# Layer norm shared between GpSimd and VectorE, value weights split first, first transposes row by row, and 28 transposes of the identity ahead of them, in a banded-attention block with a feed-forward network

## Chip, cores and metric

The kernel runs on one core of a Trainium2 chip. The metric is device time in microseconds (us); lower is better.

## The reference

The input x has 8 batches of 1024 rows of 512 numbers, in float32. Each row is normalised (no scale or shift), and two branches are added to x:

```python
xn = (x - mean) / sqrt(var + 1e-5)
Q, K, V = xn @ Wq + bq, xn @ Wk + bk, xn @ Wv + bv        # 16 heads of 64
scores = Q @ K.T; scores = where(|i - j| <= 64, scores, 0.0)
attn = softmax(scores) @ V                                 # zeros outside the band count in the softmax
s = xn @ Win + bin_                                        # 64 units
g = (relu(s[..., None] * W1 + b1) * W2).sum(-1) + b2       # 16 inner units each
out = x + attn @ Wo + bo + g @ Wout + bout
```

## The kernel before

Five engines run five hand-written instruction streams that meet only in semaphores. TensorE (PE) does matmuls and 128x128 transposes, ScalarE (ACT) and VectorE (DVE) empty PSUM, GpSimd (POOL) works SBUF to SBUF, SyncE (SP) issues all DMAs. Matmul operands are split in a high part (a rounded copy, made by ACT) and a low part (the difference, made by DVE from PSUM or by POOL from SBUF); each product is three matmuls (`PASSES`).

**Steps.** The heads are worked in 8 pairs. Step n = 8 b + k works on batch b, pair k: `project` makes the value line (V, halves 0 and 1) and the query and key lines (`project_qk`, Q and K of two halves), while the attention of the pair before (j = n - 1: scores, mask, exponentials, weights, `weigh_values`) and the output projection of the pair before that (o = n - 2, `project_out(0)` to `(7)`, L1027 to L1040) run between them. There are 64 steps and two that drain. The order within a step is written out by hand for each engine; an engine waits in order, so whatever stands behind a waiting instruction waits too.

**Opening.** SP loads the first four row tiles of batch 0 in two quarters (`x_quarter`), the value weights of pair 0, the other four row tiles as one piece (`x_in[1]`), the query and key weights, and then 18 small constants. DVE takes statistics (L701, L681) and aggregates them (`mean_and_variance`, L683). POOL's `layer_norm` (L308 to L323) makes var + eps, its power of -1/2 (L315, rstd), mean times rstd and its negative (shift), four small operations with waits between them. ACT's `normalise` (L413, L422) makes each row tile as xn = rstd x + shift. PE's `transpose_x` (L982) turns four row tiles of one of four column blocks into a PSUM bank (`XT_BANK`), ACT makes the high part of a block (`x_high`), DVE the low part (`x_low`). The order in POOL's stream is: layer norm of tiles 0 to 3, low part of V (`split_low`, L326, L328), layer norm of tiles 4 to 7, low parts of Q and K. In ACT's stream: rows 0 to 3, high part of V, rows 4 to 7, four `x_high`, high parts of Q and K. PE makes blocks 0 and 1, waits for both low parts, makes blocks 2 and 3, waits for all four low parts, and begins V projection 0.

**Weights.** In the first eight steps (`split`) the weights of the next pair are loaded raw, split by ACT and POOL, and written to a DRAM copy (`w_kept`, `wo_kept`); later steps load the split copy. The output weights of pair 7 are an exception: they are never kept, but loaded raw in step k = 7 of each batch and split again in the step k = 0 that follows (ACT L662, POOL L396). In step k = 0 of batches 1 to 7, `project_out(0)` waits for all seven writes or loads of `wo_kept` issued up to then (`wo_got`).

**Layer norm of the next batch.** DVE takes the statistics in steps k = 3 to 5 and aggregates late in step k = 5. POOL's `layer_norm` stands after the second `normalise_weights` and ahead of the weight splits and of `output_low(0)`. ACT makes row tile 0 at the end of step k = 5, between the two `output_high`, the others in steps 6 and 7. **Biases.** POOL adds bo + bout to the rows (`add_biases(p)`, L366 to L371, two tiles each): p = 0 and 1 in step k = 0, p = 2 and 3 in step k = 1, one ahead of the second group of `normalise_weights`, one between the two `output_low`.

**Waits.** Many waits on a count are written twice, once for 1 and once for the count (`in_register`).

## Time and profile before

| | us |
|---|---|
| median of 3 runs | 2365.82 |
| lowest, highest | 2365.38, 2368.52 |
| the profiled execution | 2367.19 |
| its span, first to last instruction | 2365.4 |
| TensorE busy (matmuls) | 2310.1 (98%) |
| VectorE busy | 1960.6 (83%) |
| ScalarE busy | 1576.8 (67%) |
| GpSimd busy | 892.6 (38%) |
| all DMA queues, share of 16 engines | 24% |

The mean granted TensorE clock is 0.996. A busy TensorE is not one at its peak: matmuls overlap in the pipeline, so a matmul is shown as 0.39 us long while the next one starts 0.23 us after it. The waits of an engine are read from the idle time before an instruction and the instruction whose semaphore ended it. "issue" is a wait for which the view finds no releaser. In the rows, L numbers are lines of the kernel before: L1021 projections of Q, K and V, L1038 output projection, L1009 scores, L986 transposes of the rows, L1076 transposes of the attention weights.

### The profile page before, as it was taken

What the parts mean: (1) busy time and instruction counts of PE and PEld (TensorE: products, weight loads), DVE (VectorE), ACT (ScalarE), POOL (GpSimd) and SP (SyncE); (2) the same over time, 40 slices, a digit from 0 to 9 for tenths busy, and PEclk for the clock granted to TensorE, in tenths of its full rate; (3) what the DMA queues carried; (4) which work ended last, traced back from release to release, by engine and by line L of the source; (5) the groups of instructions that cost most, each with busy time, mean ns of one, the idle gap of its engine ahead of it and who ended that gap; (6) DMA issues with size and microseconds to landing.
All of it is one profiled execution on the core that took longest, in us unless ns stands there. A gap on an engine that the chain in (4) does not pass through costs nothing.

```text
span 2365.4 us, 43885 instructions
## 1 busy us (share of the span) xinstructions
PE 2310.1 (98%) x14913; PEld 1975.8 (84%) x14913; DVE 1960.6 (83%) x5088; ACT 1576.8 (67%) x4289; POOL 892.6 (38%) x1302
## 2 busy tenths in 40 slices
PE   5999999999999999999999999999999999999996
PEld 4787888888888888888888888888888888888885
DVE  4887779887898878988889878898879888798886
ACT  3776667666676667666667666766676666676664
POOL 3544435333343324334243332443334332443332
PEclk9999999999999999999999999999999999999999
DMA  4231213221132121421223221331212311122211
GB/s 136 86 125 55 103 59 108 72 72 59 46 123 75 54 75 34 138 65 54 66 63 109 71 57 56 91 98 54 77 46 90 107 55 59 54 89 64 66 47 45
DMA packets 69501, 177.58 MB, mean 75 GB/s; under 512 B 6536, under 2 KB 18848, under 8 KB 69280
## 3 DMA queue, kind: packets, MB, share of 16 engines
q1 hardware_dynamic: 69280, 174.78, 23.6%
q8 instruction: 121, 1.98, 0.3%
q14 instruction: 100, 0.82, 0.1%
HBM read 141.73 MB, written 33.03 MB: 74 GB/s over the span
## 4 chain that ended last, share of the span: by engine, by line
PE 93%; DVE 3%; issue 2%; ACT 1%; POOL 1%; DMA 0%; POOLq 0%; SPq 0%; ACTq 0%; DVEq 0%
PE ps L1021 43%; PE ps L1038 15%; PE ps L1088 12%; PE ps L1076 9%; PE ps L1009 7%; PE ps L1066 2%; PE ps L986 1%; PE ps L1048 1%; DVE probs L733 1%; PE ps L1060 1%; DVE xn L773 1%; DVE v_back L973 0%; ACT probs L449 0%; DVE o_sum L810 0%; DMA acc<-in_L_attn_x 0%
## 5 line engine op out<-in xcount | busy, mean ns | idle before, releaser
L1021 PE MATMUL ps<-xT_hi,w_split 128*128 128x512 f32 x3072 | 1040.7, 400 | 8.1 <-POOL w_split L328 5.0
L358 POOL TENSOR_SCALAR probs<-probs,inv_l,neg_e 128x256 f32<-128x256 f32 x1024 | 569.2, 577 | 638.1 <-DVE neg_e L749 638.1
L1021 PEld LDWEIGHTS ps<-xT_hi,w_split 128*128 128x128 f32 x3072 | 578.4, 188 | 135.3 <-issue 5.2
L449 ACT ACTIVATE probs<-probs,neg_max 128x256 f32<-128x256 f32 x1024 | 507.0, 498 | 142.0 <-DVE neg_max L739 140.9
L1021 PE MATMUL ps<-xT_lo,w_split 128*128 128x512 f32 x1536 | 600.4, 391 | 0.0
L756 DVE TENSOR_TENSOR acc<-ps,acc 128x512 f32<-128x512 f32 x512 | 344.4, 685 | 164.1 <-PE ps L1038 162.6
L500 ACT ACTIVATE pT_hi<-ps 128x512 fp32r<-128x512 f32 x512 | 278.1, 599 | 225.7 <-PE ps L1088 139.5
L364 POOL TENSOR_TENSOR oT_lo<-o_sum,oT_hi 128x512 fp32r<-128x512 f32 x128 | 163.7, 1294 | 682.9 <-ACT oT_hi L516 681.9
L733 DVE CUSTOM_DVE_ANT_0 probs<-ps,mask 128x256 f32<-128x256 f32 x1024 | 372.6, 419 | 31.7 <-PE ps L1009 31.3
L800 DVE TENSOR_TENSOR pT_lo<-ps,pT_hi 128x512 fp32r<-128x512 f32 x512 | 328.2, 684 | 51.1 <-ACT pT_hi L500 50.6
L1038 PE MATMUL ps<-wo_split,oT_hi 128*128 128x512 f32 x1024 | 331.2, 405 | 12.4 <-POOL wo_split L396 5.2
L1021 PEld LDWEIGHTS ps<-xT_lo,w_split 128*128 128x128 f32 x1536 | 290.2, 189 | 51.9
L1088 PE MATMUL ps<-pT_lo,v 128*128 128x256 f32 (+1 forms) x1280 | 306.3, 280 | 0.0
L1088 PE MATMUL ps<-pT_hi,v 128*128 128x256 f32 (+1 forms) x1280 | 302.6, 275 | 0.5 <-DVE pT_lo L800 0.5
L1076 PE MATMUL ps<-ident,probs 128*128 128x128 f32 x2048 | 258.3, 273 | 4.9 <-POOL probs L358 4.0
L1076 PEld LDWEIGHTS ps<-ident,probs 128*128 128x128 f32 x2048 | 230.4, 140 | 23.3 <-issue 3.0
L1088 PEld LDWEIGHTS ps<-pT_lo,v 128*128 128x128 f32 x1280 | 244.1, 191 | 5.1
L1088 PEld LDWEIGHTS ps<-pT_hi,v 128*128 128x128 f32 x1280 | 243.1, 190 | 5.9 <-DVE pT_lo L800 0.8
L1038 PEld LDWEIGHTS ps<-wo_split,oT_hi 128*128 128x128 f32 x1024 | 182.8, 190 | 51.9 <-issue 10.2
L1038 PE MATMUL ps<-wo_split,oT_lo 128*128 128x512 f32 x512 | 201.9, 394 | 0.0
L810 DVE SCALAR_TENSOR_TENSOR o_sum<-ps,v_back,o_part 64x512 f32<-64x512 f32 x256 | 190.8, 745 | 12.9 <-ACT o_part L509 9.0
L449 ACT ACTIVATION_READ_ACCUMULATOR probs<-probs,neg_max 128x1 f32 x1024 | 192.9, 188 | 0.0
(92 smaller groups left out, 3125.1 us busy)
## 6 DMA issues: line engine op xcount, KB each, us to landing
w_split<-w_kept SPq DMA_DIRECT2D x168, 512.0 KB, 3.6
wo_split<-wo_kept SPq DMA_DIRECT2D x49, 512.0 KB, 4.4
out_x<-acc SPq DMA_DIRECT2D x16, 1024.0 KB, 5.9
acc<-in_L_attn_x SPq DMA_DIRECT2D x15, 1024.0 KB, 7.7
w_kept<-w_split SPq DMA_DIRECT2D x24, 512.0 KB, 5.5
wo_raw<-in_L_attn_Wo SPq DMA_DIRECT2D x15, 256.0 KB, 4.8
wo_kept<-wo_split SPq DMA_DIRECT2D x7, 512.0 KB, 3.0
w_raw<-in_L_attn_Wv SPq DMA_DIRECT2D x8, 256.0 KB, 5.5
```

What stands on the lines that cost most here:

```text
L358: pool.tensor_scalar(probs[:, h, t], probs[:, h, t], inv_l[:, c:c + 1], neg_e[:, c:c + 1], ALU.mult, ALU.add).then_inc(normed, 1)
L449: act.activation(probs[:, h, t], probs[:, h, t], ACT.Exp, bias=neg_max[:, c:c + 1], accum_out=row_sum[:, c:c + 1])
L500: act.activation(pT[u % 2][hi][:, c * LINE:c * LINE + LINE], ps[PT_BANK[u][c]][:], ACT.Copy) \
L733: dve.tensor_tensor_reduce(out=probs[:, h, t], in0=ps[SCORE_BANK[tp][h]][:, i * WIN:i * WIN + WIN], in1=mask[:], scale=1.0, scalar=0.0, op ...
L756: dve.tensor_tensor(acc[:, parity, t], ps[OUT_BANK[t]][:], acc[:, parity, t], ALU.add) \
L800: dve.tensor_tensor(pT[u % 2][lo][:, cols], ps[PT_BANK[u][c]][:], f32(pT[u % 2][hi][:, cols]), ALU.subtract).then_inc(pT_lo, 1)
L810: dve.scalar_tensor_tensor(o_sum[half][rows], ps[PV_BANK[u]][rows], v_back[rows], o_part[h][rows], ALU.add, ALU.add).then_inc(o_summed, 1)
L1009: last = pe.matmul(ps[SCORE_BANK[tp][h]][:, i * WIN:i * WIN + WIN], qT[qp][rows, t * P:t * P + P], kT[kp][rows, t * P:t * P + WIN], start= ...
L1021: last = pe.matmul(dst[:], w[wp][:, i, c], xT[xp][:, c, half * LINE:half * LINE + LINE], start=(c == 0 and a == 0), stop=(c == KC - 1 and ...
L1038: last = pe.matmul(ps[OUT_BANK[t]][:], oT[op][:, t * P:t * P + P], wo[wp][:], start=(a == 0), stop=(a == 2))
L1076: last = pe.transpose(ps[PT_BANK[u][c]][:, i % 4 * P:i % 4 * P + P], probs[:, h, t, i % 2 * P:i % 2 * P + P], ident[:])
L1088: last = pe.matmul(ps[PV_BANK[u]][:, q0:q0 + (end - first) * P], v[:, (4 * half + c) % T, h].rearrange("p a d -> p (a d)"), pT[h][part][:, ...
```

## The change

1. **Layer norm.** DVE makes var + eps (in `mean_and_variance`) and shift in one operation (`shift_rows`), POOL only the power (`inverse_deviation`). In batch 0 DVE also makes four of the eight row tiles (`first_rows`: 2, 3, 6, 7), ACT the others. For later batches the power moves in POOL's stream from ahead of the weight splits to behind `output_low(0)` of step k = 5, and DVE's shift stands last in that step.
2. **Opening.** The second half of batch 0 comes in two quarters. ACT splits the value weights before its first row; the high part of Q comes before rows 4 and 5, that of K after them. DVE slips the statistics of tiles 4 to 7 between the four `x_low`. PE transposes row tile by row tile, as the rows come (2, 0, 3, 1), each into four banks, and V projection 0 waits for one block's low part at a time. The mask's first memset moves ahead of the second power.
3. **28 transposes of the identity** stand on PE ahead of the first rows.
4. **Biases.** All four `add_biases` of batch 0 run in step 0.
5. **Output weights.** Those of pair 7 are split once, kept like the others and loaded from the copy; `project_out(0)` of steps up to 9 waits for the split, later ones for their own load; a load waits for the one before it.
6. **Waits** are written once. Helpers that only took register counts go.

```diff
         XT_BANK = (7, 2, 2, 4, 7, 5, 3, 2)
+        FIRST_XT_BANK = (7, 2, 0, 4)
+        WARM_UP = 28
...
             def load_output_kept(n, pair):
                 sp.wait_ge(out_done, T * (n - 1))
+                sp.wait_ge(wo_got, 16 * (n - 1))
                 sp.dma_start(f32(wo_split[:]), wo_kept[pair]).then_inc(wo_got, 16)
...
-            for i in range(2):
+            for i in range(4):
                 sp.dma_start(acc[:, 0, 2 * i:2 * i + 2], x_d[0][:, 2 * i:2 * i + 2]).then_inc(x_quarter[i], 16)
-            load_raw(V_, 0)
-            sp.dma_start(acc[:, 0, 4:T], x_d[0][:, 4:T]).then_inc(x_in[1], 16)
+                if i == 1:
+                    load_raw(V_, 0)
...
-                if k == PAIRS - 1:
-                    load_output_raw(k, PAIRS - 1 + b)
...
-                if attend and k > 0:
-                    load_output_kept(n, k - 1)
+                if n == PAIRS:
+                    keep_output(n, PAIRS - 1)
+                elif attend:
+                    load_output_kept(n, (k - 1) % PAIRS)
...
+            def inverse_deviation(tiles, done):
+                pool.wait_ge(ln_eps, done)
+                pool.tensor_tensor(rstd[:, tiles], var_eps[:, tiles], minus_half[:, tiles], ALU.pow).then_inc(ln_rstd, 1)
...
             pool.wait_ge(pool_set, 2)
-            layer_norm(0, slice(0, 4), 1, 0)
+            inverse_deviation(slice(0, 4), 1)
             split_low(0, V_)
-            layer_norm(0, slice(4, T), 2, 4)
+            pool.memset(mask[:], 1.0).then_inc(pool_set, 1)
+            inverse_deviation(slice(4, T), 2)
             split_low(0, Q_)
             split_low(0, K_)
-            pool.memset(mask[:], 1.0).then_inc(pool_set, 1)
...
                 if attend:
                     normalise_weights(0)
-                if k == 1 and proj:
+                if k == 1 and proj and b > 0:
                     add_biases(2)
                 if attend:
                     normalise_weights(1)
-                if k == 5 and not last:
-                    layer_norm(b + 1, slice(0, T), b + 3, 4 * b + 8)
                 if split_next:
                     split_low(n + 1, V_)
                     split_low(n + 1, Q_)
                 if k == 0 and proj:
                     add_biases(0)
                     add_biases(1)
+                if n == 0:
+                    add_biases(2)
+                    add_biases(3)
                 if attend:
                     output_low(0)
+                if k == 5 and not last:
+                    inverse_deviation(slice(0, T), b + 3)
-                if k == 1 and proj:
+                if k == 1 and proj and b > 0:
                     add_biases(3)
                 if attend:
                     output_low(1)
-                if attend and (split or k == 0):
-                    pool.wait_ge(wo_hi, j + 1 if split else PAIRS - 1 + b)
+                if attend and n <= PAIRS:
+                    pool.wait_ge(wo_hi, j + 1)
...
-            for t in tiles_of(0):
-                normalise(0, t, small=4 if t == 0 else None)
             split_high(0, V_)
-            for t in tiles_of(1):
-                normalise(0, t, small=8 if t == 4 else None)
+            for t in (0, 1):
+                normalise(0, t)
             for i in range(4):
                 x_high(0, i)
             split_high(0, Q_)
+            for t in (4, 5):
+                normalise(0, t)
             split_high(0, K_)
...
             for t in tiles_of(0):
...
-            mean_and_variance(tiles_of(0), 4)
-            for t in tiles_of(1):
                 statistics(0, t)
-            mean_and_variance(tiles_of(1), T)
+            mean_and_variance(tiles_of(0), 4, 1)
+            shift_rows(slice(0, 4), 1)
+            first_rows(2)
+            first_rows(3)
             for i in range(4):
+                statistics(0, 4 + i)
                 x_low(0, i)
+            mean_and_variance(tiles_of(1), T, 2)
+            shift_rows(slice(4, T), 2)
+            first_rows(6)
+            first_rows(7)
...
             pe.wait_ge(ident_set, 1)
-            for i in range(4):
-                if i == 2:
-                    pe.wait_ge(xT_lo, 2)
-                transpose_x(0, i)
+            for i in range(WARM_UP):
+                pe.transpose(ps[V_BANK[0]][:, 0:P], ident[:], ident[:])
+            for t, ready, count in ((2, xn_first, 1), (0, xn_ready, 1), (3, xn_first, 2), (1, xn_ready, 2)):
+                pe.wait_ge(ready, count)
+                for i in range(KC):
+                    last = transpose_tile(0, i, t)
+                    if t == 1:
+                        last.then_inc(xT_done, 1)
...
                     for c in range(KC):
+                        if n == 0 and i == V_ and half == 0:
+                            pe.wait_ge(xT_lo, c + 1)
...
-                    if t == 0 and split:
+                    if t == 0 and o < PAIRS:
                         pe.wait_ge(wo_lo, o + 1)
-                    elif t == 0 and k == 1:
-                        pe.wait_ge(wo_lo, PAIRS - 1 + b)
                     elif t == 0:
-                        pe.wait_ge(wo_got, 16 * (7 * b if k == 0 else 7 * b + k - 1))
+                        pe.wait_ge(wo_got, 16 * (o + 1))
```

## Rows read from the trace of the kernel before

**Rows 1.** Windows of the span: us, busy time and count of each engine, clock, DMA.

```profile
0.00:60.00 60.00, 34.38 (x167) 27.16 (x168) 26.37 (x48) 23.65 (x42) 19.54 (x29) 1.00 0.44 138
350.00:2310.00 1960.00, 1959.55 (x12732) 1680.44 (x12731) 1659.73 (x4338) 1325.95 (x3635) 723.67 (x1073) 1.00 0.23 72
```

**Rows 2.** Waits of TensorE, whole span: us in total, times, longest.

```profile
PE ps L986 <- ACT xn L422: 14.7, 1, 14.7
...
PE ps L1038 <- POOL wo_split L396: 5.2, 1, 5.2
PE ps L1021 <- POOL w_split L328: 5.0, 1, 5.0
PE ps L1076 <- POOL probs L358: 4.0, 3, 1.8
PE ps L1038 <- issue: 3.3, 2, 2.6
```

**Rows 3.** Chain that ended last, first 60 us: start, us, what.

```profile
26.80 4.61 PE ps L1021 x12
...
32.84 2.77 PE ps L1021 x12
```

**Rows 4.** Windows of TensorE alone: us, busy and count, granted clock, DMA.

```profile
74.62:78.03 3.41, 1.56 (x8) 1.00 0.01 2
...
98.50:101.90 3.40, 3.40 (x27) 0.50 0.92 268
...
235.04:238.50 3.46, 3.05 (x7) 0.51 0.00 0
```

**Rows 5.** Timeline of the opening: start us, us, engine and line, operation.

```profile
8.59 1.05 POOL L315 TENSOR_TENSOR rstd<-var_eps,minus_half 128x4 f32<-128x4 f32 x1
...
14.73 1.94 PE L986 MATMUL ps<-ident,xn 128*128 128x128 f32 x8 [14.73 <-ACT xn L422]
...
15.19 1.27 POOL L328 TENSOR_TENSOR w_split<-w_raw,w_split 128x512 fp32r<-128x512 f32 x1 [4.91 <-ACT w_split L411]
...
18.64 2.93 ACT L422 ACTIVATE xn<-acc,shift,rstd 128x512 f32<-128x512 f32 x4 [3.53 <-POOL shift L323]
```

**Rows 6.** DMA issues of 0 to 3.5 us: KB, us to landing.

```profile
w_raw<-in_L_attn_Wv SPq DMA_DIRECT2D x1, 256.0 KB, 5.6
```

**Rows 7.** Timeline of step 1: a small DVE operation, and POOL's bias additions.

```profile
71.76 2.74 DVE L744 SCALAR_TENSOR_TENSOR row_l<-e,row_sum 128x8 f32<-128x8 f32 x1 [1.11 <-ACT e L452]
...
92.39 2.99 POOL L371 TENSOR_TENSOR acc<-acc,bias_row 128x512 f32<-128x512 f32 x2
```

**Rows 8.** Timeline, end of step 5 and start of step 6.

```profile
231.46 1.96 POOL L315 TENSOR_TENSOR rstd<-var_eps,minus_half 128x8 f32<-128x8 f32 x1
...
235.45 0.77 PE L1021 MATMUL ps<-xT_hi,w_split 128*128 128x512 f32 x1 [5.03 <-POOL w_split L328]
```

**Rows 9.** Timeline of a later batch, the same place (steps 13 and 14).

```profile
528.21 0.82 ACT L422 ACTIVATE xn<-acc,shift,rstd 128x512 f32<-128x512 f32 x1 [1.27 <-POOL shift L323]
...
529.45 0.57 ACT L477 ACTIVATE vT<-ps 128x512 f32<-128x512 f32 x1
...
532.85 0.62 PE L1038 MATMUL ps<-wo_split,oT_hi 128*128 128x512 f32 x2
```

**Rows 10.** Timeline of step 8: SyncE's queue, and TensorE.

```profile
317.01 0.32 SPq L215 DMA_DIRECT2D wo_kept<-wo_split  x1
...
319.98 0.70 PE L1038 MATMUL ps<-wo_split,oT_hi 128*128 128x512 f32 x2 [0.64 <-issue]
```

**Rows 11.** Timeline of the tail.

```profile
2345.74 2.49 POOL L364 TENSOR_TENSOR oT_lo<-o_sum,oT_hi 128x512 fp32r<-128x512 f32 x2 [7.36 <-ACT oT_hi L516]
...
2349.55 1.19 PE L1038 MATMUL ps<-wo_split,oT_hi 128*128 128x512 f32 x2 [5.17 <-POOL wo_split L396]
```

**Rows 12.** DMA issues of 2316 to 2324 us: KB, us to landing.

```profile
wo_split<-wo_kept SPq DMA_DIRECT2D x1, 512.0 KB, 3.3
```

**Rows 13.** The same transfers in the view of the tile wo_split, whole span.

```profile
DMA to landing us min/median/max: 2.9/4.4/5.9
```

178 lines of the change are left out of this document (81 added, 97 removed).

## Prediction

> **What bounds the kernel now.** I read the windows first, then the waits of the matmul queue, then the chain and the timeline round each wait. From 350 to 2310 us TensorE is busy for 1959.55 of 1960.00 us, in the first 60 us for 34.38 [rows 1]. So for seven of the eight batches nothing but matmul work counts, and whatever the change takes off the other engines there is worth nothing. What can be won is the list of waits [rows 2]: 14.7 us until the first normalised rows, 5.2 us on POOL's low part of the output weights (in the tail), 5.0 us on the low part of the value weights (end of step 5), 4.0 us in three pieces on POOL's normalised weights, 3.3 us in two pieces that have no releaser in the view (2.6 of it at the start of output projection 0 of step 2, 0.6 in step 8), and others in the opening. The chain gives the two landmarks of the opening: V projection 0 starts at 26.80 and takes 4.61 us for 12 matmuls, Q projection 0 starts at 32.84 and takes 2.77 for 12 [rows 3]. The same work is 1.7 times as long before the clock is up.
>
> **The clock.** With the wait of 1.8 us in step 1 the granted clock stayed at 1.00; after the wait of 2.6 us it was 0.50 for 3.40 us, and after the wait of 5.0 us 0.51 for 3.46 us [rows 4], the lower level of 1.2 GHz. A stretch of that length at half speed costs half of it, 1.7 us. I take a removed wait of 2.6 us or more as giving back 1.7 us more, one of 1.8 us as not.
>
> **The opening.** Before: rstd runs on POOL at 8.59 for 1.05 us, shift is out at 10.3, ACT makes four rows, the first eight transposes take 1.94 us from 14.73, but POOL then spends 1.27 us from 15.19 on the value weights ahead of the second half's layer norm, and ACT makes four more rows (2.93 us from 18.64) before it copies the first transposed block [rows 5]. After: the value weights land at about 1.8 + 5.6 = 7.4 us [rows 6], ACT's table load (about 1.3) and high part (0.6) end near 9.3, rstd near 9.5. DVE's shift then meets POOL's low part of V. What two such operations do to each other is in the trace: a DVE operation of 128x8 elements took 2.74 us at 71.76, beside POOL's additions [rows 7]. I take one POOL operation of blocking, shift out at 10.8. ACT's two rows are done at 12.4, DVE's two at 11.8. The 16 transposes: at the old cold pitch (1.94 us for 8, so 0.24 each) the first block is complete at 14.6; at the warm pitch (0.11) at 12.7. I take the cold one: between the 28 transposes of the identity (from 1.6 to at latest 8.3 us at 0.24 each) and the first real one at 11.5 lie at least 3.1 idle us, more than the wait of 2.6 after which the clock fell. Copy 0.6 and subtraction 0.7 put the low part of block 0 at 16.0; the other three come 1.2 us apart, since DVE slips a statistics operation (0.6) between them: 19.6. V projection 0 ends near 21, not 31.4. The second half: aggregate 0.4, epsilon 0.2, rstd 1.05, shift again behind one POOL split (1.3), two ACT rows 0.8 each: 24.3; then ACT's K split 0.6 and its copy of the value line 0.8, which frees the bank of transposes 5: 25.7; transposes 1.0: Q projection 0 starts at 26.7 instead of 32.84, 6.1 us earlier. But V projection 0 left TensorE idle from 21 to 24.4, so the clock, which before came up during V projection 0 [rows 3], now comes up between 28 and 31 and Q projection 0 runs partly cold: 0.6 to 2.2 us, taken as 1.4. **Gain 4.7 us.** Bounds: 2.5 (both DVE operations blocked for two POOL operations each, late clock) to 10 (no blocking, warm throughout).
>
> The Trainium skill speaks against the warm-up: "TensorE: Matmul & The Clock Gate", Part 4 (PE-mode transpose), says that transposes do not count as activity for the clock as matmuls do; by it the 28 transposes leave the clock where it was, which is the cold sum above, and no row here shows a clock that rose or stayed low during transposes alone. On the blocking, the Trainium skill, "SBUF — State Buffer" (Who interferes with whom), says that a VectorE operation with two SBUF inputs and a reading GpSimd operation exclude each other for a whole instruction; the row of 2.74 us agrees, and with the rule the opening's gain is the 4.7 above, without it, two times 1.2 us more, 7.1.
>
> **Steps 0 to 2.** Four of the eight bias additions of batch 0 move from step 1 to step 0 on POOL. In step 1 two of them (2.54 us) stood ahead of the second group of normalised weights and held DVE's row_l for 2.74 us [rows 7]; without them neg_e is 2.4 us earlier and the wait of 1.8 us [rows 2] is gone: 1.8. Two others stood between the low halves of the output (2.99 us from 92.39) ahead of the low part of the output weights [rows 7], for which projection 0 of step 2 waited 2.6; without them that is 2.9 us earlier, wait and clock fall go: 2.6 + 1.7 = 4.3. The price: POOL is busy 5 us longer at the turn from step 0 to 1, and DVE's small operations (neg_max, v_back, the split of Wout) can be held there; one to two of 1.3 us reach the normalised weights. I take 1.3 (bounds 0 to 2.8). **Gain 1.8 + 4.3 - 1.3 = 4.8.**
>
> **Step 5 and 6 of batch 0.** POOL waited at layer norm of the next batch (rstd at 231.46), and only then split V for step 6; TensorE waited 5.03 us until 235.45 [rows 8]. After, the split of V comes before it. Next late is the output weight's low part: POOL does low output half 0 (to 233.7), rstd 1.96 (235.7), then DVE's shift, ACT's row (0.81), high half 1 and high part of Wo (1.1), so POOL's low half 1 and low Wo end near 240.0; projection 0 of step 6 would be due at 238.2. A new wait of 1.9 us, short enough to keep the clock. **Gain 5.0 + 1.7 - 1.9 = 4.8** (bounds 2 and 6.7).
>
> **Later batches, step 5 to 6.** The same order, without weight splits. ACT, held at the normalised row, starts at about 530.6 in place of 528.2; its line of values, at 529.45 before [rows 9], ends at 532.6, and projection 0, which needs it, starts at 532.85. DVE is 1.8 us late, its masks end at 533.2 and scores 2 wants them at 533.6. So 0.3 us of slack are left: cost 0. If the cover were gone, each tenth would count six times. Taking the kept pair 7 of Wo by DMA saves ACT and POOL work and doubles a load in these batches; TensorE waits for none of it, 0. The doubled wait instructions that go stand on engines with slack: 0 (bound 0.3).
>
> **Step 8 and the tail.** Projection 0 of step 8 waited for the write of wo_kept, issued at 317.01; it started at 319.98 [rows 10]. After, it waits for the split alone: 0.6. In the tail POOL's second low half and then its low part of Wo end before TensorE restarts at 2349.55 [rows 11]. After, the weights come by DMA, issued near 2343.3 and 3.3 us under way when nothing else is [rows 12], so 2346.6; low half 0 is out at 2345.74 + 1.3 = 2347.0, and TensorE starts near 2347.1: **gain 2.4** (0.3 if the DMA takes 5.9, its longest [rows 13]).
>
> **Sum.** 4.7 + 4.8 + 4.8 + 0.6 + 2.4 = 17.3 us. The profiled execution took 2367.2, its span 2365.4, 1.8 us lie round it; the span should become 2348.1. The median shown is 2365.8, 1.4 below the profiled one; the same difference from it gives 2348.5.
>
> **Rivals.** (B) The warm-up works: the clock is up at 11.5, the first block is ready 2.0 us earlier and all behind it: 2346.5. For it: 28 transposes keep TensorE busy for up to 6.7 us. Against: the idle time after them. Chance 0.25. (C) The slack of 0.3 us in the six later batches isn't there: POOL's rstd of 1.96 us is the longest link and one more blocked DVE operation of 1.3 us makes a wait of 1.0 in each: 6 us, 2354.5. Chance 0.15. (D) The same place, but the wait is over 2.6 us, so that the clock falls too: 6 x (2.6 + 1.7) = 26, less the gain: 2374, slower than before. It decides from a delay of 2.9 us of the value line; nothing adds up to that. Chance 0.03. (E) The opening gains nothing, because DVE carries rows, statistics and subtractions and each is held by POOL: the second half's shift at 28 in place of 22.7; 2353. Chance 0.10. The forecast (A): 0.47.
>
> **How the numbers follow.** About 0.2% (4.7 us) is what a measurement can tell from no change. A, B, C and E are faster; D is slower; some of C with E near nothing. Faster 0.95, same 0.02, slower 0.03. Range 2341 (the high bounds of opening and step 6 together, 17.3 + 5 + 2) to 2356 (C with part of E).
>
> **What would show it.** The first V projection matmul near 16 us and the first Q projection near 26.7; transposes at a pitch of 0.24 us (A) or 0.11 (B) at 11 to 15 us; no wait on w_split at step 6 and one of about 2 us on wo_split; none in step 2 and step 8; none between 350 and 2300; TensorE's last wait about 2.4 us shorter. A wait of L1038 repeated in six batches would prove me wrong through C or D; a first Q projection after 30 us through E.

## The result

The changed kernel takes 2344.44 us (median of 4 runs, 2344.23 to 2348.07) against 2366.38 us for the kernel before (2365.38 to 2368.52): a ratio of 0.9906, with a 95% interval of 0.9892 to 0.992. That is 21.9 us less, where 17.3 were forecast. The profiled execution took 2344.23 us with a span of 2342.5, against 2365.4 before, so the two traces differ by 22.9 us.

I read the trace of the changed kernel in the order of the prediction. First the windows: us, busy time and count of each engine, clock, DMA.

```profile
0.00:60.00 60.00, 47.06 (x237) 37.90 (x238) 34.75 (x82) 24.45 (x52) 23.71 (x27) 0.94 0.47 144
350.00:2290.00 1940.00, 1939.56 (x12595) 1663.67 (x12594) 1638.00 (x4295) 1307.20 (x3590) 699.22 (x1042) 1.00 0.24 74
```

From 350 us on nothing changed: TensorE is as full as before [rows 1]. In the first 60 us it is busy for 12.7 us more (28 transposes of the identity, 6.2 us, are among them). The waits of TensorE, in total, times and longest:

```profile
PE ps L1022 <- POOL oT_lo L333: 3.5, 2, 2.8
PE ps L963 <- DVE xn L664: 3.4, 1, 3.4
PE ps L963 <- ACT xn L389: 3.3, 1, 3.3
...
PE ps L1060 <- POOL probs L327: 2.2, 3, 1.1
...
PE ps L1022 <- issue: 1.4, 2, 1.2
```

Of the list before [rows 2] the 14.7 us ahead of the rows are now 1.6 ahead of the identity and 3.4 between it and the first rows, and the second half's rows have a wait of 3.3 of their own; the 5.0 on the value weights are gone, the 4.0 on the normalised weights are 2.2, and the 5.2 in the tail are 2.8, now on the output's low part (L333) and no longer on the weights.

To see where each microsecond went I measured every step on TensorE, from the first matmul of its value projection to that of the next, and the end from that of step 63 to the last matmul of the program. This is worked out from the start times of the matmuls in the traces, in us:

| kernel, profiled execution | step 1 starts | steps 1 and 2 | steps 5 and 6 | step 8 | the end |
|---|---|---|---|---|---|
| before | 55.1 | 71.5 | 78.2 | 40.9 | 75.9 |
| changed | 49.0 | 67.0 | 73.0 | 40.0 | 69.7 |
| difference | -6.1 | -4.6 | -5.2 | -0.9 | -6.2 |
| forecast | -4.7 and +1.3 | -6.1 | -4.8 | -0.6 | -2.4 |

(The forecast puts 1.3 us of price on the turn from step 0 to 1, which could fall on either side of that boundary. It fell behind it: the only wait of TensorE at the end of step 0 that the bias additions make, 1.1 us for the value line, is as long in the kernel before.) All other steps agree to 0.02 us.

**The opening.** Timeline of the changed kernel: start, us, engine and line, operation, and in brackets the idle time before it.

```profile
1.57 6.18 PE L973 MATMUL ps<-ident 128*128 128x128 f32 x28 [1.57 <-POOL ident L290]
...
8.22 1.03 POOL L295 TENSOR_TENSOR rstd<-var_eps,minus_half 128x4 f32<-128x4 f32 x1 [6.70 <-DVE var_eps L655]
9.22 1.26 POOL L299 TENSOR_TENSOR w_split<-w_raw,w_split 128x512 fp32r<-128x512 f32 x1
9.28 1.22 DVE L659 SCALAR_TENSOR_TENSOR shift<-mean_var,rstd 128x4 f32<-128x4 f32 x1 [1.22 <-POOL rstd L295]
...
11.14 3.53 PE L963 MATMUL ps<-ident,xn 128*128 128x128 f32 x16 [3.39 <-DVE xn L664]
...
14.21 2.07 ACT L395 ACTIVATE xT_hi<-ps 128x512 fp32r<-128x512 f32 x4 [2.16 <-PE ps L963]
...
15.68 0.47 PE L1007 MATMUL ps<-xT_hi,w_split 128*128 128x512 f32 x1 [1.01 <-DVE xT_lo L671]
```

Against [rows 5] the first transposes start 3.6 us earlier and the value projection 11 us earlier. The chain has query projection 0 at 25.75 instead of 32.84 [rows 3], but with 3.89 us for 12 matmuls instead of 2.77; the windows of TensorE (busy and count, clock, DMA) say why.

```profile
25.75 3.89 PE ps L1007 x12
```

```profile
7.56:10.97 3.41, 0.19 (x2) 1.00 1.14 325
10.97:14.39 3.42, 3.25 (x15) 0.50 0.31 57
14.39:24.63 10.24, 4.90 (x19) 1.00 0.67 199
24.63:28.04 3.41, 3.40 (x10) 0.50 0.72 224
...
2311.56:2314.97 3.41, 3.41 (x8) 0.50 0.00 0
```

The clock came up at 7.56, in the 28 transposes of the identity, and was down again (1.2 GHz) when the real ones ran; it came up a second time behind those, and went down behind the gap between value projection 0 and the second transposes.

**Step 5 to 6.** The wait for the value weights [rows 8] is gone. The new one is at output projection 0 of step 6, which starts 1.2 us behind the end of the matmuls before it:

```profile
223.05 1.65 POOL L295 TENSOR_TENSOR rstd<-var_eps,minus_half 128x8 f32<-128x8 f32 x1
...
224.94 0.82 ACT L389 ACTIVATE xn<-acc,shift,rstd 128x512 f32<-128x512 f32 x1 [3.20 <-DVE shift L659]
...
226.36 1.30 POOL L333 TENSOR_TENSOR oT_lo<-o_sum,oT_hi 128x512 fp32r<-128x512 f32 x1 [1.65 <-ACT oT_hi L481]
...
227.62 1.27 POOL L368 TENSOR_TENSOR wo_split<-wo_raw,wo_split 128x512 fp32r<-128x512 f32 x1
...
228.99 0.70 PE L1022 MATMUL ps<-wo_split,oT_hi 128*128 128x512 f32 x2 [1.18 <-issue]
```

In a later batch, where [rows 9] left 0.3 us of slack by my count, ScalarE's line of values ends at 515.2, 0.9 us ahead of the projection, and TensorE doesn't wait:

```profile
514.63 0.58 ACT L444 ACTIVATE vT<-ps 128x512 f32<-128x512 f32 x1
...
516.07 0.61 PE L1022 MATMUL ps<-wo_split,oT_hi 128*128 128x512 f32 x2
```

**The tail.** The load of the kept weights is issued at 2326.27 and takes 3.2 us; what TensorE waits for is the first of two low parts of the output on GpSimd. Compare [rows 11]: the same two matmuls took 1.19 us there, at half clock, and 0.70 here.

```profile
2326.27 0.32 SPq L204 DMA_DIRECT2D wo_split<-wo_kept  x1
2328.72 2.51 POOL L333 TENSOR_TENSOR oT_lo<-o_sum,oT_hi 128x512 fp32r<-128x512 f32 x2 [7.37 <-ACT oT_hi L481]
2330.13 0.70 PE L1022 MATMUL ps<-wo_split,oT_hi 128*128 128x512 f32 x2 [2.77 <-POOL oT_lo L333]
```

### The profile page after: what moved, and what is told of

It reads as the page before. It is cut to its first block, busy times and chain, and to the rows that moved or that the text cites. A ratio compares the mean times of both kernels' runs of the same rounds, so it can differ in the third digit from the quotient of the medians.

```text
span 2342.5 us, 43395 instructions
## 1 busy us (share of the span) xinstructions
PE 2311.5 (99%) x14941; PEld 1978.1 (84%) x14941; DVE 1958.1 (84%) x5110; ACT 1566.9 (67%) x4278; POOL 871.2 (37%) x1268
## 4 chain that ended last, share of the span: by engine, by line
PE 93%; DVE 4%; ACT 1%; issue 1%; POOL 0%; DMA 0%; SPq 0%; ACTq 0%; POOLq 0%
PE ps L1007 43%; PE ps L1022 15%; PE ps L1072 12%; PE ps L1060 9%; PE ps L993 7%; PE ps L1050 2%; PE ps L963 1%; PE ps L1032 1%; PE ps L1044 1%; DVE probs L710 1%; DVE xn L750 1%; DVE v_back L950 0%; DVE neg_max L716 0%; ACT probs L416 0%; DVE acc L733 0%
## 5 line engine op out<-in xcount | busy, mean ns | idle before, releaser
L333 POOL TENSOR_TENSOR oT_lo<-o_sum,oT_hi 128x512 fp32r<-128x512 f32 x128 | 163.6, 1292 | 782.2 <-ACT oT_hi L481 781.3
```

## The experiments

Each kernel is the changed one with the edit shown. The times are medians of four runs. Single runs of one kernel differ by up to 5 us (e3_split_later; 7 in e11_all_28). In the traces the clock falls at different places, and for some slower runs the mean granted clock is lower too (0.993 in the run of 2348.07 of the changed kernel, 0.996 to 0.997 in its other three). Besides, the kernel before, run again beside the experiments, had medians of 2367.4 to 2368.1 us, against the 2366.38 above. So a difference of 1 us between two medians shows nothing by itself; where that matters I read the steps of the trace instead. The steps of all kernels, counted as above:

| kernel | median us | lowest to highest | step 1 starts | steps 1, 2 | steps 5, 6 | step 8 | the end |
|---|---|---|---|---|---|---|---|
| changed | 2344.44 | 2344.23 to 2348.07 | 49.0 | 67.0 | 73.0 | 40.0 | 69.7 |
| e1_no_warm | 2344.28 | 2344.19 to 2348.53 | 49.4 | 67.0 | 72.9 | 40.0 | 73.7 |
| e2_warm_56 | 2346.04 | 2343.17 to 2347.24 | 47.9 | 67.0 | 72.9 | 40.0 | 69.8 |
| e3_split_later | 2344.36 | 2340.98 to 2345.93 | 45.8 | 68.2 | 73.0 | 40.0 | 72.5 |
| e4_bias_step1 | 2350.22 | 2349.26 to 2351.48 | 48.4 | 71.4 | 73.0 | 40.0 | 71.1 |
| e5_pow_first | 2350.37 | 2349.15 to 2352.98 | 48.6 | 68.2 | 77.3 | 40.0 | 71.1 |
| e6_tail_fill | 2344.70 | 2344.07 to 2345.18 | 48.6 | 67.0 | 73.0 | 40.0 | 69.8 |
| e7_reload_fill | 2347.31 | 2346.69 to 2348.10 | 49.5 | 67.0 | 73.0 | 40.9 | 72.2 |
| e8_block_order | 2343.50 | 2343.26 to 2345.29 | 48.2 | 67.0 | 72.9 | 40.0 | 69.8 |
| e9_bias_early | 2344.68 | 2342.70 to 2345.22 | 47.7 | 66.1 | 72.9 | 40.0 | 72.6 |
| e10_all | 2335.51 | 2335.47 to 2335.84 | 41.1 | 66.1 | 72.9 | 40.0 | 69.9 |
| e11_all_28 | 2337.36 | 2336.09 to 2343.16 | 41.4 | 66.2 | 73.2 | 40.2 | 69.9 |
| e12_row_later | 2334.77 | 2334.59 to 2336.18 | 41.0 | 66.1 | 72.0 | 40.0 | 71.5 |

### Does the warm-up do anything?

```diff
-        WARM_UP = 28
+        WARM_UP = 0
```

> The changed kernel without the 28 transposes of the identity ahead of the rows; nothing is left out of the computation. In the changed kernel's trace TensorE runs them from 1.57 to 7.75 us, the granted clock rises at 7.56, falls again at 10.97 in the gap before the first row transposes (11.14), and rises for good at 14.39. Theory (the warm-up is paid back by nothing, since the gap behind it loses the clock again): the row transposes start at 11.14 as before, cold, the clock still rises at about 14.4, and the time is 2344.4 within 0.4 us. Rival (it brings the rise at 14.39 forward, as a head start): without it the clock rises one record later, at about 17.8, the first half of the value projection runs cold for some 2 us of its 4.4, and the time is about 2345.5. A third, that the warm-up is in the way of something: 2343.5 or less.

2344.28 us, the same. The row transposes start at 11.12 and are cold as before (16 in 3.65 us), the clock comes up at 15.36, just ahead of the value projection at 15.62. The theory holds for the changed kernel's trace: its 28 transposes bring nothing, since the clock that they brought up at 7.56 fell again in the idle time behind them. It isn't so in every execution: in three later traces with 28 transposes (e3_split_later, e9_bias_early, e11_all_28) the clock stayed up to 11.25, 11.77 and 11.94 us, over idle times of 3.8 to 4.5 us, and the first of the real transposes ran warm. Then with as many as fill that gap:

```diff
-        WARM_UP = 28
+        WARM_UP = 56
```

> The changed kernel with 56 transposes of the identity in place of 28; nothing is left out. At full clock one transpose follows the other in 0.108 us, so 28 more end at about 10.8, just ahead of the first rows at 11.1. Theory (transposes of fp32 do raise and hold the clock, as the rise at 7.56 suggests, and the gap alone lost it): no half clock from 7.6 to the end of the value projection; the 16 row transposes take 4 x 0.43 after each row instead of 0.21 each, the last block is complete at about 12.6 instead of 14.6, the value projection starts at about 14.0 instead of 15.68, and the time is 2342.7 (2342.2 to 2343.2). Rival (transposes don't count as activity; the rise at 7.56 had another reason): the clock falls or stays low, the row transposes keep their 0.213 us, and the time is 2344.4, or up to 2 us more if the added transposes at half clock (0.213 each) run past 11.1.

Timeline of TensorE, and its windows with the clock:

```profile
1.57 8.91 PE L973 MATMUL ps<-ident 128*128 128x128 f32 x56 [1.57 <-POOL ident L290]
10.96 1.97 PE L963 MATMUL ps<-ident,xn 128*128 128x128 f32 x16 [0.47 <-DVE xn L664]
14.10 0.47 PE L1007 MATMUL ps<-xT_hi,w_split 128*128 128x512 f32 x1 [1.18 <-DVE xT_lo L671]
```

```profile
6.90:20.56 13.66, 9.56 (x62) 1.00 0.69 209
20.56:27.38 6.82, 5.36 (x16) 0.50 0.86 280
```

The mechanism is as the theory has it: 56 transposes take 8.91 us where 28 took 6.18, the clock stays up through them, the 16 row transposes take 1.97 us instead of 3.53, and the value projection starts at 14.10 instead of 15.68. The time is not: 2346.04 against the 2342.7 expected. In the trace step 1 starts 1.1 us earlier, not 1.6, because the stretch at half clock behind the value projection is now 6.8 us long instead of 3.4; and two of the four runs are near 2347.2, 4 us over the fastest, by as much as the ends in the table differ; their mean granted clock is 0.995, that of the other two 0.997. So a warm-up of the right length makes the transposes warm, but no gain in time is shown: the median came out above the expected range.

### What GpSimd's split costs beside VectorE's shift

```diff
+            pool.wait_ge(xn_first, 2)
             split_low(0, V_)
             pool.memset(mask[:], 1.0).then_inc(pool_set, 1)
             inverse_deviation(slice(4, T), 2)
+            pool.wait_ge(xn_first, 4)
             split_low(0, Q_)
```

> The changed kernel with GpSimd's low parts of the value and query weights held back until VectorE has done its two normalised rows of the same half; nothing is left out. In the changed kernel's trace the shift of 4 columns takes 1.22 us in both halves, from the start of GpSimd's split beside it to its end, where the same instruction took 0.17 elsewhere. Theory (the 1.05 us is the port that the two engines share, and it is on the path): the shift takes 0.17 in both halves, the rows start 1.0 earlier, the value projection starts at about 14.7 and query projection 0 at 23.3 instead of 25.4; the time is 2342.4 (2342.0 to 2343.0). If the clock's rise at 14.39 doesn't move forward with the work, the first half's gain is kept all the same, since the value projection would begin after it. Rival (the shift is long for a reason of its own, such as waiting for GpSimd's pow result to land): the shift stays at 1.2 and the time at 2344.4. Second rival (the split, now late, is waited for by the value projection or the query projection): 2344.4 to 2346.

```profile
9.24 0.17 DVE L661 SCALAR_TENSOR_TENSOR shift<-mean_var,rstd 128x4 f32<-128x4 f32 x1 [1.22 <-POOL rstd L295]
...
10.52 1.28 POOL L299 TENSOR_TENSOR w_split<-w_raw,w_split 128x512 fp32r<-128x512 f32 x1 [1.32 <-DVE xn L666]
...
48.47 1.59 DVE L696 CAST wout_hi<-wout_raw 128x512 fp32r<-128x512 f32 x1
```

The shift takes 0.17 us instead of 1.22, and 0.16 in the second half: what held it was the split beside it, and not the power's result, which comes to it as before. Query projection 0 starts at 22.10 instead of 25.40, more than the 2.1 us expected, and step 1 3.2 us earlier. Of these 3.3 us about 1.1 lie in each half's shift, and 1.0 are the clock's, not the edit's: in this execution it stayed up until 11.25 us, and the 16 row transposes took 2.57 us instead of 3.53. And 1.2 us are lost again in step 1, which took 32.97 us against 31.75. The same happened in e5_pow_first (32.94), which has the changed kernel's opening, so the edit isn't the cause. The traces differ in one VectorE operation beside GpSimd's bias additions: the copy `wout_hi` took 0.41 us in the changed kernel and 1.59 in these two, and TensorE's wait for the first group of normalised weights was 0.9 us there and 2.0 in these. In this execution the clock was at half level for 6.8 us in the tail; the fastest run, 2340.98, is 3.3 us under the fastest of the changed kernel, the medians are equal. By its time alone this run would be inconclusive; its trace is not.

### The order of the first transposes

```diff
-            for t, ready, count in ((2, xn_first, 1), (0, xn_ready, 1), (3, xn_first, 2), (1, xn_ready, 2)):
-                pe.wait_ge(ready, count)
-                for i in range(KC):
-                    last = transpose_tile(0, i, t)
-                    if t == 1:
-                        last.then_inc(xT_done, 1)
+            for i in range(KC):
+                transpose_x(0, i)
```

> The changed kernel with the first 16 row transposes block by block, as in the kernel before, instead of row by row; nothing is left out. Row by row they run from 11.14 to 14.6 us at 0.213 each, and no block is complete before the last row's four, 13.96 at the earliest; block by block they can't start before the last row is normalised, at 12.05, but the first block is complete 4 transposes later. After that VectorE's pace of 1.2 us a block sets the value projection's matmuls either way. Theory: block by block is the better order here: the first high part starts at about 12.95 to 13.3 instead of 14.21, the value projection at 14.5 to 14.8 instead of 15.68, the time is 2343.4 (2343.0 to 2343.8) if the clock behaves alike. Rival (row by row hides the transposes behind the rows and is worth its place): the fourth block is complete at 15.5 instead of 14.6 and the time is 2345.2.

2343.50 us, 0.9 less than the changed kernel, where the rival would have 0.8 more; the size is read from the trace.

```profile
12.24 3.68 PE L963 MATMUL ps<-ident,xn 128*128 128x128 f32 x16 [4.91 <-ACT xn L389]
13.39 0.60 ACT L395 ACTIVATE xT_hi<-ps 128x512 fp32r<-128x512 f32 x1 [1.21 <-PE ps L963]
...
24.59 0.78 PE L1003 MATMUL ps<-xT_hi,w_split 128*128 128x512 f32 x1
```

The transposes start 1.1 us later (12.24 against 11.14), but ScalarE has its first complete block at 13.39 instead of 14.21, and query projection 0 starts at 24.59 instead of 25.40. Row by row no block is complete until the last row is; this part of the change costs 0.8 us.

### The bias additions

```diff
-                if k == 1 and proj and b > 0:
+                if k == 1 and proj:
                     add_biases(2)
 ...
-                if n == 0:
-                    add_biases(2)
-                    add_biases(3)
 ...
-                if k == 1 and proj and b > 0:
+                if k == 1 and proj:
                     add_biases(3)
```

> The changed kernel with the bias additions of rows 2, 3, 6 and 7 of batch 0 back in step 1, where the kernel before has them; nothing is left out. Theory (GpSimd's queue in step 1 is what made TensorE wait at the end of steps 1 and 2 in the kernel before): the waits of about 1.8, 2.6 and 1.7 us come back and the short one of step 1 (network and bias work beside each other) goes: the time is 2348.9 (2347.5 to 2349.7), 4.5 more. Rival (the gain of steps 1 and 2 came from the other edits, such as the mask being set earlier or the shorter layer norm on GpSimd): 2344.4 to 2345.4.

2350.22 us, 0.5 above the range. In the trace, 5.1 us longer than the changed kernel's, steps 1 and 2 take 4.5 us more, as expected, and the end 1.3 more, with 3.4 us at half clock in it; step 1 starts 0.6 earlier. GpSimd's queue in step 2 and what waits for it, as in [rows 7]:

```profile
87.06 2.99 POOL L340 TENSOR_TENSOR acc<-acc,bias_row 128x512 f32<-128x512 f32 x2
...
91.23 1.27 POOL L365 TENSOR_TENSOR wo_split<-wo_raw,wo_split 128x512 fp32r<-128x512 f32 x1
...
92.59 0.70 PE L1019 MATMUL ps<-wo_split,oT_hi 128*128 128x512 f32 x2 [2.66 <-issue]
```

The waits are those of the kernel before, but the clock fell behind the other one. The wait in step 1, with the window of TensorE right behind it (busy and count, clock, DMA):

```profile
70.90 1.01 PE L1057 MATMUL ps<-ident,probs 128*128 128x128 f32 x4 [1.87 <-POOL probs L327]
71.00:74.41 3.41, 3.41 (x17) 0.50 0.00 0
```

Behind the 2.66 us the clock stayed at 1.00. So step 1 is 1.3 us longer than in the kernel before (33.99 against 32.65) and step 2 1.4 us shorter (37.43 against 38.88). The sum of the two steps is 71.4, against 71.5 before, and holds one stretch at half clock either way.

The other way, all eight additions as early as they can be:

```diff
+                if n == 0:
+                    for p in range(4):
+                        add_biases(p)
                 if split_next:
                     split_low(n + 1, V_)
                     split_low(n + 1, Q_)
-                if k == 0 and proj:
+                if k == 0 and proj and n > 0:
                     add_biases(0)
                     add_biases(1)
-                if n == 0:
-                    add_biases(2)
-                    add_biases(3)
```

> The changed kernel with all eight bias additions of batch 0 ahead of GpSimd's splits of step 1's weights instead of behind them; nothing is left out. In the changed kernel GpSimd stands idle from 27.4 to 41.2 us and then adds from 45.0 to 56.2, beside VectorE's work on the first scores. Theory (GpSimd's late additions are what is left of TensorE's waits in steps 1 and 2, partly by its own turn, partly by holding VectorE's small operations): the additions run from 27.5 to 38.7, the softmax weights of step 1 are normalised earlier, TensorE's waits of 0.6 and 1.2 us in step 1 and of 0.4 in step 2 go; step 1 takes about 29.9 us instead of 31.75 (or 32.95, as in two of the kernels so far) and the time is 2342.1 (2341.5 to 2343). Rival (the additions, now beside VectorE's low parts of queries and keys, hold that engine in step 0, which takes longer by as much): 2344 or more.

```profile
26.70 10.02 POOL L340 TENSOR_TENSOR acc<-acc,bias_row 128x512 f32<-128x512 f32 x8
...
59.70 4.78 POOL L327 TENSOR_SCALAR probs<-probs,inv_l,neg_e 128x256 f32<-128x256 f32 x8 [8.38 <-DVE neg_e L726]
```

The additions run where they were meant to, and VectorE's small operations get short (neg_max 0.17 us instead of 1.01, the low part of Wout 0.69 instead of 1.67). But step 1 takes 30.85 us instead of 31.75, 0.9 less and not 1.8, and step 2 is unchanged: the size expected there was wrong by half. Another 1.3 us, not counted on, are gained at the end of step 0: the last key projection starts at 44.0 us in both traces and step 1 at 47.7 instead of 49.0, since TensorE's wait of 1.1 us for the value line is gone. GpSimd now stands idle for 8.38 us ahead of the normalised weights, waiting for VectorE, and TensorE still waits 1.1 us for the second group of them: what is left is VectorE's chain and the 4.8 us that GpSimd then normalises, not the additions. The time, 2344.68 (2344.73 in the profiled execution), doesn't show the gain; in the trace 6.8 us at half clock stand against it in the tail, and 6.8 instead of 3.4 in the opening behind the value projection.

### The place of the inverse deviation

```diff
+                if k == 5 and not last:
+                    inverse_deviation(slice(0, T), b + 3)
                 if split_next:
                     split_low(n + 1, V_)
 ...
-                if k == 5 and not last:
-                    inverse_deviation(slice(0, T), b + 3)
```

> The changed kernel with GpSimd's inverse deviation of the next batch put back ahead of the weight splits of step 5, where the kernel before has its layer norm; nothing is left out. Theory (in the kernel before, the low parts of step 6's weights came late because GpSimd stood waiting for VectorE's means and variances): TensorE waits again for the low part of the weights at the start of step 6, some 4 us in step 5 or 6 (less than the 5.2 that went, since GpSimd now has one operation there instead of four), and the 1.35 us wait at output projection 0 of step 6 shrinks or goes: 2347.5 us (2346.5 to 2349). Later batches split nothing and stay as they are. Rival (the wait went because the layer norm on GpSimd became short, not because of its place): 2344.4 to 2345.

```profile
221.10 2.08 POOL L295 TENSOR_TENSOR rstd<-var_eps,minus_half 128x8 f32<-128x8 f32 x1 [11.38 <-DVE var_eps L655]
223.16 2.50 POOL L299 TENSOR_TENSOR w_split<-w_raw,w_split 128x512 fp32r<-128x512 f32 x2
224.57 0.47 PE L1007 MATMUL ps<-xT_hi,w_split 128*128 128x512 f32 x1 [4.00 <-POOL w_split L299]
```

The wait is back at 4.0 us, with the clock's fall behind it (225.3 to 228.7), and the one at output projection 0 is gone: steps 5 and 6 take 4.4 us more. So the place does it; the kernel before took 0.9 us more in these two steps, and that is the most that the shorter layer norm can have saved. The time, 2350.37, is 1.4 above the range: in the trace 1.2 us more in step 1 (the copy `wout_hi`, as in e3_split_later) and 1.3 in the tail have nothing to do with the edit.

### The tail: split or clock?

Transposes of the identity in TensorE's two waits at the end, and the same with the output weights of pair 7 read raw and split in each batch as the kernel before does (44 in place of 24):

```diff
+                if n == B * PAIRS + 1:
+                    for _ in range(24):
+                        pe.transpose(ps[4][:, 0:P], ident[:], ident[:])
 ...
+                if n == B * PAIRS:
+                    pe.wait_ge(v_lo, 2 * j + 2)
+                    for _ in range(16):
+                        pe.transpose(ps[6][:, 0:P], ident[:], ident[:])
```

The reload, in e7_reload_fill alone (with the conditions on GpSimd, ScalarE and TensorE that belong to it):

```diff
+                if k == PAIRS - 1:
+                    load_output_raw(k, PAIRS - 1 + b)
 ...
-                if n == PAIRS:
-                    keep_output(n, PAIRS - 1)
-                elif attend:
-                    load_output_kept(n, (k - 1) % PAIRS)
+                if attend and k > 0:
+                    load_output_kept(n, k - 1)
```

> The changed kernel with transposes of the identity added in TensorE's two waits after the last step: 16 ahead of the third tile of the output projection of step 64 (bank 6) and 24 ahead of the first of step 65 (bank 4); nothing is left out. So far the part from the last step's value projection to the last matmul took 75.9 us in the kernel before (10.2 us at half clock in it), and 69.7 in the changed one; in four executions of near kernels the same program there took 69.8, 71.1, 72.5 and 73.7, with 3.4, 3.4, 6.8 and 13.6 us at half clock. Theory (the only difference is where the clock's fall lands against the 2.9 us wait; transposes in the waits hold the clock): no half clock after 2300 until the last matmul, 69.7 us or up to 0.3 less in every execution, and the times lie within 0.4 us of each other at about 2344.1, without the 2348 that was among the changed kernel's. Rival (transposes don't hold the clock): times as before, 2344.3 to 2348. Second rival (the added transposes delay the projection): 2345 or more.

> The changed kernel with the output weights of pair 7 read raw and split again in each batch, as in the kernel before, and with transposes of the identity in the waits of the end, 16 and here 44 ahead of the last output projection, to hold the clock; nothing is left out. Theory (of the 6.2 us that the end got shorter, 2.4 are GpSimd's split of those weights and the rest is the clock, which fell in the 5.2 us wait): the wait is 2.4 us longer than with the kept weights and the clock stays up, so the end takes 72.1 us and the time is 2346.5 to 2347 (in the middle batches, at most 0.9 us more in step 8). Rival (the whole 6.2 us come from the split, by the wait and what follows it): 2350.3. Second rival (a reload in every batch costs in the later batches too, 0.3 us or more in each): 2348.5 or more.

Windows of TensorE with the clock, e6_tail_fill first, then e7_reload_fill, and the tail of the latter:

```profile
2300.00:2341.20 41.20, 31.07 (x225) 1.00 0.22 77
```

```profile
2300.00:2343.20 43.20, 35.05 (x257) 1.00 0.12 43
```

```profile
2332.62 1.28 POOL L367 TENSOR_TENSOR wo_split<-wo_raw,wo_split 128x512 fp32r<-128x512 f32 x1
2334.00 0.69 PE L1023 MATMUL ps<-wo_split,oT_hi 128*128 128x512 f32 x2 [0.38 <-issue]
```

With the clock held in both, the end takes 69.8 us with the kept weights and 72.2 with the reload: 2.4 for the split. The kernel before, with the reload and 10.2 us at half clock, took 75.9: 3.7 for the clock. The first rival (all of it the split) would have needed 75.9 here, and falls; so does the second, since no step from 9 to 62 differs by more than 0.04 us; step 8 alone takes 0.85 us more. The reload costs 2347.31 - 2344.70 = 2.6 us at the median, where 2.4 + 0.85 = 3.3 were in the traces. One part of the expectation failed: the four times of e6_tail_fill lie 1.1 us apart, not 0.4, so the tail was not the only place where executions differ. The stretch at half clock at 2311.56 in the changed kernel cost nothing: 69.7 with it, 69.8 without.

### Together

e10_all has the early additions, the split behind the rows, a mixed order of the first transposes (blocks 0 and 1 row by row for rows 2, 0 and 3, the rest block by block), GpSimd's low part of the query weights ahead of the second inverse deviation, ScalarE's value copy ahead of rows 4 and 5, statistics of rows 4 and 5 ahead of the first low part, and transposes of the identity in four gaps of TensorE: 48, 20, 16 and 24.

```diff
-        WARM_UP = 28
+        WARM_UP = 48
 ...
+            pool.wait_ge(xn_first, 2)
             split_low(0, V_)
             pool.memset(mask[:], 1.0).then_inc(pool_set, 1)
-            inverse_deviation(slice(4, T), 2)
             split_low(0, Q_)
+            inverse_deviation(slice(4, T), 2)
 ...
                         pe.wait_ge(xT_lo, 1)
+                        for _ in range(20):
+                            pe.transpose(ps[6][:, 0:P], ident[:], ident[:])
```

> The version that the runs point to, with nothing left out: the bias additions early; GpSimd's low part of the value weights only after VectorE's two rows and that of the query weights ahead of the second inverse deviation; the first transposes of blocks 0 and 1 row by row for rows 2, 0 and 3, and the rest block by block; statistics of rows 4 and 5 ahead of the first low part; ScalarE's value copy ahead of rows 4 and 5 and its copy of the key weights behind the first two high parts of the second half; 48 transposes of the identity at the start, 20 between the value projection and the second transposes, 16 and 24 in the waits of the end. Theory (the port, the order and the clock each give what the runs so far show): the first rows at 9.45 instead of 10.53, the clock full from the warm-up on, the value projection from about 12.8 instead of 15.7, query projection 0 from about 20.3 instead of 25.4 and not at half clock, step 1 and 2 some 2 us shorter, the end at 69.8: 2336.5 (2335.5 to 2338), all runs within 1 us. Rival (the clock falls all the same in the stretches of transposes): 2338 to 2340. Second rival (the early additions and the earlier start meet on VectorE): 2340 or more.

e11_all_28 is the same without the filling of the opening:

```diff
-        WARM_UP = 48
+        WARM_UP = 28
 ...
-                        for _ in range(20):
-                            pe.transpose(ps[6][:, 0:P], ident[:], ident[:])
```

> The previous kernel of this call with the 28 transposes of the identity at the start as in the changed kernel, and without the 20 ahead of the second transposes: all its moves, but no holding of the clock in the opening; nothing is left out. Theory (transposes in the gaps hold the clock, and the clock is worth what half clock costs there): half clock comes back for 7 to 14 us of the first 30, the value projection's first half or query projection 0 run cold, 1.5 to 3.5 us more than with them, differing from run to run: 2339 (2338 to 2340.5). Rival (the added transposes do nothing): the same time as with them, within 0.4 us.

```profile
1.57 8.40 PE L980 MATMUL ps<-ident 128*128 128x128 f32 x48 [1.57 <-POOL ident L290]
...
12.98 0.47 PE L1017 MATMUL ps<-xT_hi,w_split 128*128 128x512 f32 x1 [0.52 <-DVE xT_lo L673]
```

```profile
7.65:2332.12 2324.47, 2309.30 (x14994) 1.00 0.24 77
```

2335.51 us, 8.9 under the changed kernel (ratio to the kernel before 0.9867, interval 0.9851 to 0.9884), with the four runs within 0.4 us: the clock is up from 7.65 us to the last matmul in the trace, where query projection 0 starts at 20.05. Without the filling of the opening (e11_all_28) the median is 1.9 us higher, under the expected range, and the runs are 7 us apart, but its two fastest are only 0.6 and 0.8 above the fastest of e10_all. Its trace loses the clock once, from 11.94 to 15.35. In that execution the granted clock was 0.95 where it is 1.00 in the others, and from the start of step 1 to that of step 63 it took 7.2 us more than e10_all, nearly all of the distance of its 2343.16. So the filling is worth 0.6 to 1.9 us by these four runs, at the low end of what was expected.

The last run takes e10_all and moves one row of ScalarE's in step 5 of batch 0:

```diff
-                if ln_next and k == 5:
+                if ln_next and k == 5 and b > 0:
                     normalise(b + 1, 0)
 ...
                     act.activation(wo[hi][:], wo_raw[:], ACT.Copy).then_inc(wo_hi, 1)
+                if ln_next and n == 5:
+                    normalise(b + 1, 0)
```

> The kernel of run e10_all with one edit more: in step 5 of batch 0 ScalarE normalises row 0 of the next batch behind its high parts of the outputs and of the output weights instead of ahead of them; nothing is left out. In step 6 of batch 0 the changed kernel has a wait of 1.3 us at output projection 0, at 227.7 to 229.0 us: GpSimd's inverse deviation (1.65 us from 223.05), VectorE's shift, ScalarE's row (0.82 from 224.94), its high part of the outputs (225.66), and only then GpSimd's two low parts (226.36 and 227.62). Theory (the wait is this chain through ScalarE's row, not GpSimd's 1.65 us alone): without the row in it the two low parts run from about 224.7 to 227.3 of that trace, ahead of where TensorE comes to them; the wait goes, step 6 takes 37.1 us instead of 38.4, and the time is 2334.2 (2333.9 to 2334.6). Rival (GpSimd's deviation alone holds them long enough): 0.4 us or less of it goes, 2335.1 or more.

```profile
219.12 0.72 PE L1034 MATMUL ps<-wo_split,oT_hi 128*128 128x512 f32 x2 [0.18 <-ACT vT L442]
```

2334.77 us, 0.2 above the range and 0.7 less than e10_all, with step 6 shorter by 0.95: the chain through ScalarE's row was the wait, as the theory has it, but not the full 1.3; what is left before the projection is 0.2 us on ScalarE's value line, which the longer wait had covered. Its profiled execution, 2336.18, lost the clock once in the tail, between the added transposes, for 3.4 us, and its end is 71.5 against 69.9; the other three runs lie within 0.4 us of each other. This is the fastest version that was run.

## Why the prediction was right, point by point

**Sign and size.** The time lies within the range, 4.1 us under the point. Two terms were too small, the opening's by 1.4 and the tail's by 3.8; the rest fit to 0.4. The number alone would speak for rival B, whose 2346.5 is nearer; it is the landmarks in the trace that decide for A.

**The opening: 4.7 forecast, 6.1 to the start of step 1.** The trace has the mechanism of the sum: cold transposes, each shift blocked by one GpSimd split (1.22 and 1.22 us where 0.17 would do), low parts 1.2 us apart, clock late on query projection 0 (3.89 - 2.77 = 1.1 us, taken as 1.4). What was mis-sized are durations: rstd ends at 9.25, not 9.5, the transposes run at 0.21 to 0.22 us a piece, not 0.24, and value projection 0 ends at 20.1, not 21. They add up to query projection 0 at 25.75 instead of 26.7; these 1.0 us and the 0.3 that the clock cost less make 1.3 of the 1.4. How the 6.1 us divide among the moves of the opening (rows shared with VectorE, value weights first, quarters, one block's low part at a time) is not shown: no run takes one of them back. Only the order of the transposes (0.8 us lost), GpSimd's split beside the shift (1.1 us lost in each half) and the warm-up were tried alone. The upper bound of 10 was too low for what the opening holds: e10_all starts step 1 at 41.1, 14.0 us ahead of the kernel before.

**The warm-up.** The forecast took it at nothing because of the gap behind it, and e1_no_warm, with its equal median and cold transposes, agrees. That the gap was long enough was in part luck: the changed kernel's trace lost the clock in 3.4 us of idle time, e3_split_later, e9_bias_early and e11_all_28 kept it over 3.8 to 4.5 us into the real transposes. The Trainium skill, "TensorE: Matmul & The Clock Gate", Part 4 (PE-mode transpose), says that a transpose doesn't count as busy in the way that a matmul does and that the full clock doesn't engage for it; by it e2_warm_56 would have kept cold row transposes and 2344.4. The measurement decides otherwise here: with nothing but transposes on TensorE the clock was up at 7.56, and in e2_warm_56 the 16 row transposes took 1.97 us instead of 3.53. The sum was right for the reason that the idle time gave, not for the page's.

**The block.** The Trainium skill, "SBUF — State Buffer" (Who interferes with whom), has a VectorE operation with two SBUF inputs and a reading GpSimd operation exclude each other for a whole instruction. Here the trace agrees: 1.22 us with GpSimd's split beside it, 0.17 when that waits.

**Steps 1 and 2: 4.8 forecast, 4.6 (0.9 and 3.7).** e4_bias_step1 gives 4.5 back for this edit alone. The wait of 1.8 us is gone, as forecast. The price stands in step 1 as a new wait of 0.9 us ahead of the first group of normalised weights, made as the forecast said: VectorE's neg_max and its split of Wout are held beside GpSimd's additions (1.01 and 1.67 us), and e9_bias_early, which moves the additions away, gives these 0.9 us back. Step 2 is 3.7 us shorter where 4.3 were counted; two waits of 0.2 us each are left there.

**Steps 5 and 6: 4.8 forecast, 5.2.** The wait of 5.03 us and the clock's fall behind it went; the new wait is 1.2 us instead of 1.9; GpSimd's inverse deviation, on its chain, took 1.65 us, not 1.96. e5_pow_first puts the old wait back by the place alone, e12_row_later takes most of the new one away.

**Step 8: 0.6 forecast, 0.9.** e7_reload_fill, with the write of the kept weights back in its old place and TensorE behind it, gives 0.85 back.

**The tail: 2.4 forecast, 6.2.** This is the step that failed. The term for the wait was right to the tenth (e6_tail_fill and e7_reload_fill: 69.8 and 72.2), but the sum puts the clock at nothing here without a reason. It counts the clock's fall with the waits of steps 2 and 6 and not with this one, the longest of them (5.2 us). Nor would its rule have given the size: by it the wait that is left, 2.8 us, loses the clock as well. The window of before has 10.2 us at half clock there, 7.8 of them busy:

```profile
2347.89:2358.13 10.24, 7.80 (x18) 0.50 0.03 11
```

That is 3.7 us by e7_reload_fill's end against that of before. It is not given back in every execution: behind the wait that is left, 2.8 us, the clock may fall or not. Of the seven other traces with this tail and without added transposes in it, two (e2_warm_56, e8_block_order) kept it there, and e1_no_warm, e3_split_later, e4_bias_step1, e5_pow_first and e9_bias_early lost it for 10.2, 6.8, 3.4, 3.4 and 6.8 us. That the changed kernel's profiled execution kept it is luck that the forecast doesn't explain: with the end of e1_no_warm (73.7) the tail would have gained 2.2.

**The rule for the clock.** The prediction takes a wait of 2.6 us or more as losing the clock and one of 1.8 us as not, from one trace. The length alone doesn't decide. In e4_bias_step1 the clock fell behind the 1.87 us in step 1 and not behind the 2.66 in step 2, the other way round from the kernel before; in the changed kernel it fell at 2311.56, behind a wait of 1.95 us. The sum over steps 1 and 2 came out all the same, because one of the two waits lost the clock in either trace and neither is left.

**The rivals.** B (the warm-up works) and E (the opening gains nothing) fell with the trace and e1_no_warm. C and D fell with the trace: no step from 9 to 62 changed by more than 0.02 us. The slack of 0.3 us was an underestimate: ScalarE's line of values ends 0.9 us ahead of the projection.

## What to carry to other kernels

Count the clock with each wait that an edit removes or makes, also in the last microseconds, and as a range: behind the same wait it fell in one execution and not in the next. Small transposes in four gaps made the four runs of e10_all agree within 0.4 us; in e12_row_later, with the same ones, one run of four was still 1.6 us over the fastest. A warm-up is worth something for certain only if it lasts until the real work starts. Where two engines share the work on a short chain, keep the long GpSimd operation out of the gap between two small VectorE ones: held back by a wait it cost nothing, let loose it cost 1.05 of its 1.26 us.

## What was not expected of the hardware

- Transposes of a 128x128 identity in fp32, and nothing else, brought TensorE's clock up (at 7.56, 6.90 and 7.65 us in the changed kernel, e2_warm_56 and e10_all, from a start at 1.57; without them, in e1_no_warm, it came up at 15.36). In the gaps they held it: 2324 us in e10_all without a fall, though e12_row_later has one. They follow each other at 0.21 us at 1.2 GHz and at 0.11 at 2.4 GHz.
- The moment at which the clock comes up differs between executions of the same opening: the first rise was between 4.42 us (e3_split_later) and 7.56 (the changed kernel) in the nine traces that begin with 28 or 56 transposes and have the changed kernel's start, the work before it being the same. The same holds for its fall: after the same wait of 2.8 us in the tail it stayed up in three traces and fell for 3.4 to 10.2 us in five. The ends in the table scatter with it, from 69.7 to 73.7 us.
- Step 1 of batch 0 has two lengths, 31.75 and 32.95 us, with GpSimd's additions beside VectorE's operations. In the two long ones (e3_split_later, e5_pow_first) VectorE's copy `wout_hi`, which reads one tile, took 1.59 us, in the short ones 0.41; the difference is about the length of one GpSimd operation (1.28 us). What decides between the two was not tried; with the additions earlier the copy took 0.41 and the step 30.85, 30.85 and 30.88 us (e9, e10 and e12).
